# Row maxima taken in halves of 512 keys, scores in bursts of three, heads turned into one bank

## The reference

```python
xn = layernorm(x)                                   # x: 1024 tokens x 512, fp32
q = rope(xn @ wq + bq)                              # 32 heads of 16
k = rope(xn @ wk + bk); v = xn @ wv + bv            # 8 kv heads of 16, each for 4 query heads
scores = einsum('bqhd,bkhd->bhqk', q, k) / 4        # 32 x 1024 x 1024, not causal
s = einsum('bhqk,bkhd->bqhd', softmax(scores), v).reshape(B, S, E)
z = xn @ W.T + b                                    # feed-forward gate, 512 x 512
m = sum_e p_e * (xn @ A[e]) @ B[e]                  # 8 experts of rank 16
gamma = min(0.5 * |z| / (|m| + 1e-6), 1)
out = x + s * silu(z + gamma * m)
```

## Time and profile before

| | |
|---|---|
| time, median of 3 runs | 493.56 us (493.24 to 493.92) |
| the profiled execution's own time | 492.73 us |
| its span in the profile | 490.9 us |
| PE busy | 459.1 us, 94% |
| DVE busy | 373.0 us, 76% |
| ACT busy | 300.6 us, 61% |
| POOL busy | 88.2 us, 18% |

### The profile page before, as it was taken

One profiled execution on the slowest core, in us unless ns is written; L12 is line 12 of the kernel. 1 busy time (PEld: TensorE's weight loads), 2 busy tenths in 40 slices (PEclk: granted clock), 3 DMA queues, 4 the chain that ended last, 5 costly groups with the idle time before them and its releaser, 6 DMA issues.

```text
span 490.9 us, 7226 instructions
## 1 busy us (share of the span) xinstructions
PE 459.1 (94%) x2469; PEld 187.7 (38%) x2469; DVE 373.0 (76%) x401; ACT 300.6 (61%) x593; POOL 88.2 (18%) x159
## 2 busy tenths in 40 slices
PE   8897999999999999999999999999999999999995
PEld 3573344443333333333333333333334333333331
DVE  6544788888988888898888888888888888334331
ACT  2210001236878787787878787787877787554474
POOL 8572223341010001001000100010010001013441
PEclk9999999997999999999999999999999999999999
DMA  8999944540000000000000000000000000020110
GB/s 268 281 125 126 121 66 67 76 66 1 1 1 1 3 1 3 1 1 1 1 3 0 3 0 3 1 1 3 0 3 0 3 0 3 2 76 0 39 29 29
DMA packets 13354, 17.32 MB, mean 35 GB/s; under 512 B 3088, under 2 KB 7440, under 8 KB 13328
## 3 DMA queue, kind: packets, MB, share of 16 engines
q1 hardware_dynamic: 11808, 15.84, 17.3%
q10 hardware_dynamic: 1520, 1.12, 0.8%
HBM read 6.72 MB, written 2.10 MB: 18 GB/s over the span
## 4 chain that ended last, share of the span: by engine, by line
PE 67%; ACT 16%; SPq 4%; DVE 4%; issue 4%; DMA 4%; POOL 0%; ACTq 0%; DVEq 0%
PE oT L859 26%; PE st L896 24%; ACT arena L545 16%; PE st L739 5%; PE sm L799 3%; PE sm L877 3%; SPq L290 2%; DMA kA<-arena 2%; PE sm L868 2%; DVE negmax L614 2%; DMA idb_sb<-in_identb 2%; PE oT L739 2%; SPq L258 1%; PE sm L880 1%; SPq L264 1%
## 5 line engine op out<-in xcount | busy, mean ns | idle before, releaser
L614 DVE TENSOR_REDUCE negmax<-sm 128x1 f32<-128x1024 f32 x256 | 303.4, 1220 | 50.0 <-PE sm L799 49.8
L545 ACT ACTIVATE arena<-st 128x512 f32<-128x512 f32 x512 | 266.1, 602 | 92.1 <-PE st L896 91.5
L896 PE MATMUL st<-qA,kA 50*128 50x512 f32 x512 | 192.6, 451 | 19.2 <-ACT arena L545 11.6
L799 PE MATMUL sm<-kA,qA 48*128 48x512 f32 x512 | 200.8, 466 | 3.8 <-DMA kA<-arena 3.4
L896 PEld LDWEIGHTS st<-qA,kA 50*128 50x128 f32 x512 | 85.4, 185 | 176.6 <-ACT arena L545 158.6
L859 PE MATMUL oT<-arena,vg 128*32 128x512 f32 x1024 | 138.1, 612 | 0.0
L799 PEld LDWEIGHTS sm<-kA,qA 48*128 48x128 f32 x512 | 84.7, 185 | 28.0 <-issue 12.6
L383 POOL TENSOR_TENSOR maxp<-negmax,consts 128x16 bf16<-128x16 f32 x16 | 3.4, 214 | 239.5 <-DVE negmax L614 239.5
L471 ACT ACTIVATE arena<-arena 128x512 fp32r<-128x512 f32 x10 | 6.3, 631 | 56.5 <-POOL arena L346 56.5
L859 PEld LDWEIGHTS oT<-arena,vg 128*32 128x32 f32 x1024 | 20.3, 108 | 31.4 <-ACT arena L545 24.7
L693 DVE TENSOR_TENSOR xT_sb<-sm,b_sb 128x512 f32<-128x512 f32 x4 | 2.8, 692 | 23.6 <-PE sm L880 23.6
(11 more groups left out here) (88 smaller groups left out, 248.5 us busy)
## 6 DMA issues: line engine op xcount, KB each, us to landing
qA<-arena SPq DMA_DIRECT2D x48, 128.0 KB, 5.1
x_sb<-in_x SPq DMA_DIRECT2D x8, 256.0 KB, 5.9
kA<-arena SPq DMA_DIRECT2D x12, 128.0 KB, 6.8
wT_sb<-in_wT SPq DMA_DIRECT2D x1, 1024.0 KB, 9.4
out<-x_sb SPq DMA_DIRECT2D x1, 896.0 KB, 4.0
out<-x_sb SPq DMA_DIRECT2D x4, 224.0 KB, 1.9
z_sb<-in_wq SPq DMA_DIRECT2D x1, 768.0 KB, 10.3
wkv<-in_wk ACTq DMA_DIRECT2D x1, 256.0 KB, 4.3
```

Of the source, the lines that this page charges most:

```text
L545: act.activation(probs[:, s % PB, h, :], st[:, (st_score(0, s, h) - late) % 3, :], ACT.Exp, scale=float(D) ** -0.5).then_inc(st_free, 1)
L614: dve.tensor_reduce(negmax[:, half, r:r + 1], sm[:, bank, :], AX.X, ALU.max, negate=True).then_inc(sm_free, 1)
L799: mm = pe.matmul(sm[:, bank, kh * HALF:(kh + 1) * HALF], qA[rows, half, g // 2, h, qt * P:(qt + 1) * P], kA[rows, g // 2, kh * HALF:(kh + ...
L896: pe.matmul(st[:, (st_score(0, s, h) - fewer) % 3, :], kA[rows, g // 2, kt * P:(kt + 1) * P], qA[rows, half, g // 2, h, :], start=True, st ...
```

## The change

It has four parts.

1. **Maxima.** `sm` becomes a ring of four single banks. `row_max` reduces 512 keys and gives its bank back at once; `neghalf` keeps the two halves of a row, and `both_halves`, once for each half of the queries, takes the smaller of the two negated maxima (128x16). GpSimd waits for it (`max_both`). The rows of group 0, among the projections, are still reduced with 1024 keys (`first_row_max`). VectorE's loop over groups 1 to 6 is written out.
2. **Bursts.** A group's 64 scores are issued in bursts of three pairs (each half of 32 ends with one of two), and a block of `values` stands behind each burst, two bursts late. A half has 11 bursts and 11 blocks: the first and the last key tile are whole, and each two of the six between are cut into three blocks of 384, 128 + 256 and 256 queries (`CUTS`).
3. **Heads** are turned into one bank instead of a buffer of two, behind the block of values instead of ahead of it, and at places of the new order; the turned maxima have such places too.
4. **Group 7** has its late products one or two at a time, behind 12 of its first bursts.

```diff
-ST_PER, SM_PER = 66, 34
-MAX1_SLOT, MAX0_SLOT = 2, 10
-OUT1_SLOT, OUT0_SLOT = 2, 10
+ST_PER, SM_PER = 66, 66
+MAX1_AT, MAX0_AT = 9, 41
+OUT1_AT, OUT0_AT = 12, 44
+BURST, LAG = 3, 2
+BURSTS = -(-REP * NT // BURST)
+BLOCKS = 2 + 3 * (NT - 2) // 2
+CUTS = ((0, 0, 384), (0, 384, HALF), (1, 0, 256), (1, 256, HALF))
...
+LATE_UNITS = {2: [(4, 0), (4, 1)], 5: [(4, 2), (4, 3)], 8: [(4, NE)], 11: [(5, 0)], 14: [(5, 1), (5, 2)],
+              17: [(5, 3), (5, NE)], 20: [(6, 0), (6, 1)], 23: [(6, 2), (6, 3)], 26: [(6, NE), (7, 0)],
+              29: [(7, 1), (7, 2)], 31: [(7, 3)], 34: [(7, NE)]}
...
-        sm = ctx.enter_context(nc.psum_tensor("sm", [P, 2, S], F32))
+        sm = ctx.enter_context(nc.psum_tensor("sm", [P, 4, HALF], F32))
...
+            def row_max(g, j, count):
+
+                n, e = sm_score(g, j), j // 2
+                dve.wait_ge(sm_full, n + 1)
+                dve.tensor_reduce(neghalf[:, e // 16, e % 16, j % 2:j % 2 + 1], sm[:, n % 4, :], AX.X, ALU.max,
+                                  negate=True).then_inc(sm_free, count)
+
+            def both_halves(g, half):
+
+                dve.wait_ge(sm_free, sm_score(g, 32 * half + 31) + 1)
+                dve.wait_ge(max_parts, 2 * g + half + 1)
+                dve.tensor_tensor(negmax[:, half, :], neghalf[:, half, :, 0], neghalf[:, half, :, 1],
+                                  ALU.min).then_inc(max_both, 1)
...
-            step(0, first=True)
-            with dve.Fori(1, LAST) as g:
-                step(g)
+                both_halves(g, 1)
+
+            group(0, first=True)
+            for g in range(1, LAST):
+                group(g)
...
+                if n >= 4:
+                    pe.wait_ge(sm_free, n - 3)
+                pe.matmul(sm[:, n % 4, :], qA[rows, half, g // 2, h, qt * P:(qt + 1) * P],
+                          kA[rows, g // 2, kh * HALF:(kh + 1) * HALF], start=True, stop=True).then_inc(sm_full, count)
...
+                for kt, first_col, end_col in block_parts(b):
+                    cols = slice(first_col, end_col)
+                    for h in range(REP):
+                        mm = pe.matmul(oT[h * VC:(h + 1) * VC, cols], vg[:, g % 2, kt, :],
+                                       probs[:, (NT * half + kt) % PB, h, cols],
+                                       start=(kt == 0), stop=(kt == NT - 1))
                 mm.then_inc(pv_done, 1)
...
+                    if not last:
+                        score_rows(g + 1, i, sm_score(g, i), 2 if first and i == OUT1_AT - 1 else 1)
+                    if i % (REP * NT) % BURST != BURST - 1 and i % (REP * NT) != REP * NT - 1:
+                        continue
+                    if burst >= LAG:
+                        values(g, half, burst - LAG)
+                    elif half == 1:
+                        values(g, 0, burst - LAG + BLOCKS)
                     elif not first:
+                        values(g - 1, 1, burst - LAG + BLOCKS)
+                    if i == OUT1_AT - 1 and not first:
+                        turn_heads(1, SM_LAST["out1"] if last else sm_out1(g), 2 if last else 1, 2 * g)
```

More of the change, by code:

```diff
@@ L94, in st_max1, with block_parts, blocks_through @@
 def st_max1(g):
-    return ST_PER * g + 4 * MAX1_SLOT
+    return ST_PER * g + MAX1_AT
 def st_max0(g):
-    return ST_PER * g + 4 * MAX0_SLOT + 1
+    return ST_PER * g + MAX0_AT + 1
+def block_parts(b):
+    if b in (0, BLOCKS - 1):
+        return [(0 if b == 0 else NT - 1, 0, HALF)]
+    two, third = (b - 1) // 3, (b - 1) % 3
+    return [(1 + 2 * two + kt, a, z) for kt, a, z in ((CUTS[0],), CUTS[1:3], CUTS[3:])[third]]
+def blocks_through(g, s):
+    kt = s % NT
+    return 2 * BLOCKS * g + BLOCKS * (s // NT) + (1 + (3 * kt + 1) // 2 if kt < NT - 1 else BLOCKS)
@@ L102, in sm_base, with sm_score @@
 def sm_base(g):
[L103 to L108, removed]
+    return 64 + SM_PER * g
+def sm_score(g, j):
+    return sm_base(g) + j + (1 if j >= OUT1_AT else 0) + (1 if j >= OUT0_AT else 0)
 def sm_out1(g):
-    return sm_base(g) + OUT1_ROWS
+    return sm_base(g) + OUT1_AT
 def sm_out0(g):
-    return sm_base(g) + OUT0_ROWS + 1
+    return sm_base(g) + OUT0_AT + 1
@@ L378, in maxima @@
             def maxima(half, count, filled, emptied_by):
-                pool.wait_ge(sm_free, filled)
+                if count <= 2:
+                    pool.wait_ge(sm_free, filled)
+                else:
+                    pool.wait_ge(max_both, filled)
                 if emptied_by is not None:
@@ L908, in step @@
                         turn_maxima(st[:, st_max1(0) % 3, :], 1).then_inc(st_full, 1)
-                    if s == MAX0_SLOT and not last:
+                    if i == MAX0_AT and not last:
                         pe.wait_ge(max_parts, 2 * g + 3)
@@ L922, in step @@
[L922 to L931 removed]
+                    fewer = 1 if last and i >= MAX0_AT else 0
@@ new lines, in group @@
+                    n = st_score(g, s, h) - fewer
+                    if first and i < 3:
+                        claim_bank(i)
+                    else:
+                        pe.wait_ge(st_free, n - 2)
+                    pe.matmul(st[:, n % 3, :], kA[rows, g // 2, kt * P:(kt + 1) * P], qA[rows, half, g // 2, h, :],
+                              start=True, stop=True).then_inc(st_full, 1)
+                    if not last:
+                        score_rows(g + 1, i, sm_score(g, i), 2 if first and i == OUT1_AT - 1 else 1)
@@ L943, in _ @@
             for g in range(1, LAST):
-                step(g)
-            step(LAST, last=True)
-            for at in range(16 - LAG, 16):
-                values(LAST, at, st_score(LAST, at, 3), None)
-            turn_heads(1, SM_LAST["tail"] % 2, 2 * LAST + 2, SM_LAST["tail"] - 1)
+                group(g)
+            group(LAST, last=True)
+            for b in range(BLOCKS - LAG, BLOCKS):
+                values(LAST, 1, b)
+            turn_heads(1, SM_LAST["tail"], 2, 2 * LAST + 2)
 def kernel(L0_attn_x, L0_attn_wq, L0_attn_bq, L0_attn_wk, L0_attn_bk, L0_attn_wv, L0_attn_bv,
```

229 lines of the change are left out of this document (94 added, 135 removed).

## The result

| | before | after |
|---|---|---|
| median | 493.52 us (4 runs) | 462.34 us (4 runs, 460.22 to 464.08) |
| ratio, 95% interval | | 0.9366 (0.9325 to 0.9406) |
| span of the profiled execution | 490.9 | 462.3 |

What follows compares the result with a forecast made beforehand. No engine was full: scores waiting for the third `st` bank bounded the kernel. Fourteen halves saving 16.0 us and group 7 saving 5.8 gave 21.8 off; the forecast was 471.5 us, range 462 to 486.

Steps and rivals of the forecast that it cites:

- The wait for the third bank: Before the change, four scores between two blocks do not fit three `st` banks, costing 0.36 us of TensorE's time a slot.
- A half: 21.0 forecast: Groups 0 to 6: VectorE's 20.7 us and 0.3 of waiting, instead of 22.14; fourteen halves save 16.0.
- VectorE, up to 1.3 behind TensorE, stands some 0.1 to 0.5 in front of the division: At a half's turn, heads behind the block make VectorE wait for them; 0.3 us a half was added.
- TensorE: 20.5 forecast: TensorE's work in a half: bursts 10.9 us, values 8.7, turned heads and maxima 0.92.
- so the 0.36 a slot goes: With bursts of three, each third score starts at or behind 2.12 us, when its `st` bank is free.
- One of the signs set for being wrong: The prediction is wrong if TensorE waits for `sm` and ScalarE in the same burst.
- Group 7: 58.0 forecast: Second score to end of values: TensorE's work 57.4 us plus waits behind the small block, against 63.8; saves 5.8.
- Dearer pieces: Rival, 0.15: pieces of values have a fixed part of 0.2 us, TensorE becomes the bound; 484.9 us.
- dearer reductions: Rival, 0.05: a VectorE reduction of 512 takes 0.65 us, a half 22.3; 490.4 us.
- reductions that do not overlap: Rival, 0.08: each short VectorE reduction takes its whole 0.69 us, a half 23.6; 508 us.
- bursts that do not remove the wait: Rival, 0.04: values wait for exponentials of the burst before, a half stays at 22; 486 to 493 us.
- The rings run freer: Rival, 0.12: no wait at the division, reductions at 0.59 us, a half of 20.2; 460 to 464 us.

Runs made afterwards that it cites:

- the run with the heads ahead: The changed kernel with the heads turned ahead of the burst's block of values instead of behind it; 460.7 us, ratio 0.932 to the kernel before.
- with VectorE's limit out of the way: The changed kernel with reductions of 256 of each bank's 512 keys, half of the keys left out of the maxima; 454.1 us, ratio 0.917 to the kernel before.

## Why the prediction was right

**The wait for the third bank** was the mechanism, and it held: the chain of a slot is untouched when only the reductions change, and TensorE's and VectorE's work close up when the bursts come with them. The sum missed by 9.4 us, and it is in groups 0 to 6: 26.05 + 0.37 measured, 16.0 forecast. That the result lies inside the range at all is luck: two of the four executions (461.87 and 460.22) lie below 462, and the profiled one had lost some 3 us to the clock ahead of group 0.

**A half: 21.0 forecast, 20.23 measured.** Three terms of VectorE were too large.

- Reductions start 0.599 apart and not 0.61: 0.35 a half.
- `both_halves` was counted at 0.37 in the mean. The next reduction starts 0.67 behind the one ahead of it where one reduction stands between (257.37 to 258.04), and 0.81 in the other half (276.96 to 277.77), instead of 0.60: 0.14 in the mean. I priced it like a reciprocal (0.25; it is 0.18 long), and the wait of 0.15 for the reduction ahead is 0.03 in the rows (277.64 to 277.67). 0.23 a half.
- "VectorE, up to 1.3 behind TensorE, stands some 0.1 to 0.5 in front of the division", counted at 0.3, is the lost overlap of 0.08 that the run with the heads ahead shows. 0.22 a half.

The division itself was right, 0.86 (244.54 to 245.40) for 0.85. The sum is then 32 x 0.599 + 0.86 + 0.08 + 0.14 = 20.25. The twelve halves from group 0's division to group 6's saved 1.90 each, 22.8 us. The other two halves' worth of groups 0 to 6 saved 3.3: from group 0's first score to its division 1.4 (31.53 to 30.14; the division starts at 141.28 before and 143.34 after), and from group 6's division to group 7's first score 1.9 (13.94 to 12.04). The first of these was at a mean granted clock of 0.89 before and 0.94 after, so that how much of the 1.4 is the change's is open.

The Trainium skill's price was a rival: "VectorE: DVE Perf Modes", in the table of its section on the TRN2 errata, has 120 cycles beside the elements for an operation from PSUM, at 0.96 GHz. An estimate from it is 0.66 us for 512 elements. The trace does not agree: 0.599 from start to start, and 1.14 for 1024. The duration of one reduction, 0.683, is nearer to it, but what a full engine pays is the distance.

**TensorE: 20.5 forecast, 19.69 measured with VectorE's limit out of the way.** The blocks of one piece were right (0.78 and 0.57 for 0.78 and 0.56). The second piece of a block costs nothing: 0.79 for 128 + 256, where I had 0.90. So the fixed part belongs to the block, not to the piece. And I took 0.44 from the last pair to the block out of a row in which that pair had waited; without a wait it is 0.32. On the other side, "so the 0.36 a slot goes" was too strong: behind the small block 0.3 of it stays when VectorE's limit is away (0.19 at the third score and 0.11 at the block). One of the signs set for being wrong did show for this reason: in the changed kernel's burst behind the block at 252.55, TensorE waits for ScalarE's bank (253.46 to 253.78 instead of 0.23) and then for VectorE's (253.78 to 253.92). It did no harm there, since VectorE had rows to go on with.

**Group 7: 58.0 forecast, 58.2 measured.** Saved 5.6 for 5.8, but this closeness is in part luck. The sum has the 22 blocks of two halves; in that stretch stand 24, since group 6's last two (256 and 512 wide) come two bursts late: 0.57 + 1.0 too little. Against that, the values were counted too dear by 0.3 a half, a burst by 0.02 twenty times, and turned maxima and heads by 0.3 together. The wait behind the small block was right in size and came twice instead of three times: 0.22 at 446.89 and at 451.94.

**The rivals.** Dearer pieces, dearer reductions and reductions that do not overlap are all excluded by the rows above, and bursts that do not remove the wait by a half of 20.23. "The rings run freer" gave 460 to 464 from a half of 20.2 with chance 0.12, and that is what happened, for the reasons that it named, cheaper reductions and next to no wait at the division, and for a third that it did not, a cheaper `both_halves`.

**What I did not see** is how much the two parts need each other in groups 0 to 6. The prediction treats single banks as a cost (1.3 us of VectorE's work a half) beside the bursts' gain. The bursts alone make these groups slower; the extra work is what buys the gain.

What stays open: whether all of the 1.7 us between the medians is due to the heads ahead of the block; the halves account for 1.3, and the two intervals overlap. And no run takes the parts of the new order (three pairs to a burst, cut blocks, the places of the heads) away from each other with the old reductions, so that which of them costs the 9 us there is argued from the rows and not shown.

## What to carry to other kernels

A ring's step matters as much as its size: four banks given back one at a time fed the engine that two pairs of the same banks starved, though the single steps cost 5% more work (32 x 0.599 against 16 x 1.14). Fit a burst to the number of buffers of the ring that its consumer gives back (three pairs for three banks), and check every other ring that the same burst passes; two changes that are each worth nothing or less can be one change worth 6%. When a profile shows one engine without a gap, ask with a run that halves its work how near the next limit is before spending effort on it: here it was 0.5 us of 20.

## What the runs showed of the hardware

Short reductions overlap with each other as well as long ones: 0.683 long and 0.599 apart for 512 fp32 from PSUM, 1.22 and 1.14 for 1024, the same 0.08. Column-tiled fp32 matmuls of 128 and of 256 columns in a row, 16 rows of them, take as long as 8 of 384 (0.79 and 0.78): this split by columns within a block costs nothing. And the time of this kernel varies by 4 us between runs of one chip with the mean granted clock (460.22 at 0.995, 464.08 at 0.978), and the slowest of the four starts group 0 3.45 us later than the profiled execution before, behind a stretch of the projections with the clock at 0.65 instead of 0.91.
